# Gathering TensorE's waits and moving kept's products and the state sum in a two-stage GRU attention kernel

## The reference, cut to what is computed

```python
# first recurrence, B = 512, T = 1024, U = 64
z = sigmoid(x@Wxz + h@Whz + b); r = sigmoid(x@Wxr + h@Whr + b)
hh = relu(x@Wxh + b_in + r * (h@Whh + b_rec)); h = z*h + (1-z)*hh
logit[b, t] = sum_u(outs[t, b, u] * qw[b, u]);  a = softmax(logit, over t)
# second recurrence, its x are the first one's outs
r = sigmoid(x@Wxr + h@Whr + b); c = relu(x@Wxc + b + r * (h@Whc))
h = (1-a)*h + a*c
```

## Time and profile before

| | us |
|---|---|
| median of 3 runs (4725.99 to 4726.48) | 4726.17 |
| the profiled execution, its own time | 4727.85 |
| its span | 4726.0 |
| TensorE matmul busy | 4648.7 (98%) |
| VectorE busy | 4188.5 (89%) |
| GpSimd busy | 3629.2 (77%) |
| ScalarE busy | 2353.4 (50%) |

### The profile page before, as it was taken

How to read it: one execution, slowest core, us unless ns; L and a number is a source line. 1 busy time by engine, 2 the same in 40 slices (tenths; PEclk the granted TensorE clock), 3 DMA queues, 4 the chain that set the end, 5 groups by cost and what they waited for, 6 DMA issues and landing times.

```text
span 4726.0 us, 366111 instructions
## 1 busy us (share of the span) xinstructions
PE 4648.7 (98%) x131196; PEld 4341.8 (92%) x131196; DVE 4188.5 (89%) x28719; ACT 2353.4 (50%) x9363; POOL 3629.2 (77%) x8204
## 2 busy tenths in 40 slices
PE   8999999999999999999998999999999999999999
PEld 8999999999999999999997999999999999999998
DVE  8999999999999999999997888888888888888888
ACT  5555555555555555555553333333333333333333
POOL 6777777777777777777776888888888888888888
PEclk9999999999999999999999999999999999999999
DMA  3333333333333333333334554555555555555554
GB/s 103 107 107 114 110 107 113 110 107 111 113 107 111 113 107 108 115 108 107 115 116 119 124 122 118 124 123 119 122 124 119 121 124 120 120 124 120 119 124 108
DMA packets 169276, 544.15 MB, mean 115 GB/s; under 512 B 31644, under 2 KB 38060, under 8 KB 169260
## 3 DMA queue, kind: packets, MB, share of 16 engines
q1 hardware_dynamic: 169260, 543.93, 43.7%
HBM read 405.24 MB, written 138.56 MB: 115 GB/s over the span
## 4 chain that ended last, share of the span: by engine, by line
PE 98%; issue 1%; DMA 0%; DVE 0%; POOL 0%; SPq 0%; ACT 0%; POOLq 0%; ACTq 0%; DVEq 0%
PE r_bank_a L531 14%; PE r_bank_b L531 13%; PE c_bank_b L531 12%; PE c_bank_a L531 11%; PE logit_bank L583 6%; PE z_bank_a L537 6%; PE r_bank_a L537 5%; PE z_bank_b L537 5%; PE z_bank_a L531 5%; PE r_bank_b L537 5%; PE z_bank_b L531 4%; PE c_bank_b L537 3%; PE c_bank_a L537 3%; PE c_bank_a L543 1%; PE c_bank_b L543 1%
## 5 line engine op out<-in xcount | busy, mean ns | idle before, releaser
L295 POOL TENSOR_TENSOR kept<-z_gate,h 128x128 f32<-128x128 f32 x2048 | 931.8, 455 | 694.5 <-ACT z_gate L348 683.3
L316 POOL TENSOR_TENSOR a_kept<-attn_rest,state 128x128 f32<-128x128 f32 x2048 | 932.3, 455 | 276.7 <-POOL state L311 162.7
L311 POOL TENSOR_TENSOR state<-a_new,a_kept 128x128 f32<-128x128 f32 x2048 | 933.2, 456 | 122.0 <-DVE a_new L514 65.7
L285 POOL TENSOR_TENSOR prod<-h,qw 128x128 f32<-128x128 f32 x2050 | 933.6, 455 | 0.0
L537 PE MATMUL r_bank_a<-x,weights 64*64 64x128 f32 x8200 | 895.0, 288 | 14.0 <-ACT r_gate L377 7.9
L583 PE MATMUL logit_bank<-prod,row_sum 64*64 64x128 f32 x8208 | 895.3, 287 | 0.6 <-POOL prod L285 0.6
L537 PE MATMUL r_bank_b<-x,weights 64*64 64x128 f32 x8192 | 893.8, 288 | 0.0
L537 PE MATMUL z_bank_a<-x,weights 64*64 64x128 f32 x8200 | 876.4, 280 | 0.0
L537 PE MATMUL z_bank_b<-x,weights 64*64 64x128 f32 x8192 | 871.2, 278 | 0.2 <-DVE vec_bank L505 0.2
L444 DVE SCALAR_TENSOR_TENSOR vec_bank<-vec_bank,z_rest 128x64 f32<-128x64 f32 x4096 | 735.2, 225 | 0.3 <-issue 0.3
L455 DVE TENSOR_TENSOR h<-vec_bank,kept 128x64 f32<-128x64 f32 x4096 | 720.5, 218 | 0.3 <-issue 0.2
(11 more groups left out here) (119 smaller groups left out, 19328.3 us busy)
## 6 DMA issues: line engine op xcount, KB each, us to landing
x<-in_keys_t SPq DMA_DIRECT2D x512, 256.0 KB, 3.7
gru_outputs<-h SPq DMA_DIRECT2D x256, 512.0 KB, 3.3
x<-gru_outputs SPq DMA_DIRECT2D x512, 256.0 KB, 3.7
attn<-attention SPq DMA_DIRECT2D x512, 256.0 KB, 4.3
logits<-logit_rows SPq DMA_DIRECT2D x258, 8.0 KB
time_rows<-logits SPq DMA_DIRECT2D x2, 896.0 KB, 6.3
attention<-time_rows SPq DMA_DIRECT2D x2, 896.0 KB, 5.9
weights<-in_weight_columns SPq DMA_DIRECT2D x2, 176.0 KB, 3.7
```

Source lines behind the costliest of these rows:

```text
L285: nc.gpsimd.tensor_tensor(prod[:, (s - 1) % BODY, gcols(g)], h_at(s - 1)[:, gcols(g)], qw[:, gcols(g)], ALU.mult).then_inc(prod_ready[g], 1)
L295: nc.gpsimd.tensor_tensor(kept[:, g], z_gate[:, g], h_at(s - 1)[:, gcols(g)], ALU.mult).then_inc(kept_ready[g], 1)
L311: nc.gpsimd.tensor_tensor(state[:, (s - 1) % 2, gcols(g)], a_new[:, (s - 1) % 2, gcols(g)], a_kept[:, (s - 1) % 2, gcols(g)], ALU.add).the ...
L316: nc.gpsimd.tensor_tensor(a_kept[:, s % 2, gcols(g)], attn_rest[:, s % 2, gcols(g)], state[:, (s - 1) % 2, gcols(g)], ALU.mult).then_inc(a ...
```

## The change

In the first recurrence the slot's order becomes: [prod, xr, xz, r_ready of o, h] product for r, `gru_x_r(o)`, product for z | [z_rest of o, xh] product for the candidate, `gru_x_z(o)`, logit | [cand of o] `gru_x_h(o)`. The wait for `logits_copied` at s == 2, g == 0 stands at the front of the slot, before h's. `gru_gated` waits for rh_summed first, `gru_cand` no longer for xh_summed. In the second recurrence the slot becomes: [ar_ready of o, anew] a_new's product for r, `agru_x_r(o)`, a_new's candidate product | [axr, agated and akept of o] a_kept's two products of o | [acand of o] `agru_x_c(o)`. VectorE works in whole groups of 128 columns, and makes the state sum of the other group between gated and cand; GpSimd keeps the product alone.

```diff
@@ -303,23 +303,14 @@
                 product(BODY, g)
 
             with pool.Fori(0, T, BODY) as t0:
-                soon = t0 + 1
                 for s in range(BODY):
-                    due, soon = soon, t0 + (s + 2)
+                    done, due = t0 + (s + 1), t0 + (s + 2)
                     for g in GROUPS:
-                        pool.wait_ge(anew_ready[g], due)
-                        nc.gpsimd.tensor_tensor(state[:, (s - 1) % 2, gcols(g)], a_new[:, (s - 1) % 2, gcols(g)],
-                                                a_kept[:, (s - 1) % 2, gcols(g)], ALU.add).then_inc(s_ready[g], 1)
-                        pool.wait_ge(s_ready[g], due)
+                        pool.wait_ge(s_ready[g], done)
                         if g == 0:
-                            pool.wait_ge(rest_ready, soon)
+                            pool.wait_ge(rest_ready, due)
                         nc.gpsimd.tensor_tensor(a_kept[:, s % 2, gcols(g)], attn_rest[:, s % 2, gcols(g)],
                                                 state[:, (s - 1) % 2, gcols(g)], ALU.mult).then_inc(akept_ready[g], 1)
-            for g in GROUPS:
-                pool.wait_ge(anew_ready[g], T + 1)
-                pool.wait_ge(akept_ready[g], T + 1)
-                nc.gpsimd.tensor_tensor(state[:, (T - 1) % 2, gcols(g)], a_new[:, (T - 1) % 2, gcols(g)],
-                                        a_kept[:, (T - 1) % 2, gcols(g)], ALU.add).then_inc(s_ready[g], 1)
 
         @block.scalar
...
 
             def gru_gated(due, s, g):
+                dve.wait_ge(rh_summed[g], due)
                 dve.wait_ge(r_ready[g], due)
-                dve.wait_ge(rh_summed[g], due)
                 for part, c in PARTS:
                     nc.vector.tensor_tensor(gated[:, g, c], hid_part(g)[:, c], r_gate[:, g, c],
                                             ALU.mult).then_inc(gated_ready[g][part], 1)
@@ -430,8 +422,6 @@
                 cand, _ = vec_parts(g)
                 for part, c in PARTS:
                     dve.wait_ge(gated_ready[g][part], due)
-                    if part == 0:
-                        dve.wait_ge(xh_summed[g], due)
                     nc.vector.tensor_tensor(cand[:, c], inp_part(g)[:, c], gated[:, g, c],
                                             ALU.add).then_inc(cand_ready[g][part], 1)
...
@@ -492,37 +482,43 @@
             def agru_gated(due, s, g):
                 dve.wait_ge(ar_ready[g], due)
                 dve.wait_ge(rc_summed[g], due)
-                for part, c in PARTS:
-                    nc.vector.tensor_tensor(gated[:, g, c], c_bank[g][:, c], r_gate[:, g, c],
-                                            ALU.mult).then_inc(agated_ready[g][part], 1)
+                nc.vector.tensor_tensor(gated[:, g], hid_part(g), r_gate[:, g], ALU.mult).then_inc(agated_ready[g], 1)
 
             def agru_cand(due, s, g):
                 cand, _ = vec_parts(g)
-                for part, c in PARTS:
-                    dve.wait_ge(agated_ready[g][part], due)
-                    if part == 0:
-                        dve.wait_ge(axc_summed[g], due)
-                    nc.vector.tensor_tensor(cand[:, c], z_bank[g][:, c], gated[:, g, c],
-                                            ALU.add).then_inc(acand_ready[g][part], 1)
+                dve.wait_ge(agated_ready[g], due)
+                dve.wait_ge(axc_summed[g], due)
+                nc.vector.tensor_tensor(cand, z_bank[g][:, 0:GC], gated[:, g], ALU.add).then_inc(acand_ready[g], 1)
 
             def agru_new(due, pairs, s, g):
                 cand, _ = vec_parts(g)
-                for part, c in PARTS:
-                    dve.wait_ge(acand_ready[g][part], due)
-                    if part == 0 and g == 0 and s % CHUNK == 0:
-                        dve.wait_ge(a_loaded[s // CHUNK], pairs)
-                    last = nc.vector.scalar_tensor_tensor(a_new[:, s % 2, gcols(g)][:, c], cand[:, c], 0.0,
-                                                          attn_at(s)[:, gcols(g)][:, c], ALU.max, ALU.mult)
-                last.then_inc(anew_ready[g], 1)
+                dve.wait_ge(acand_ready[g], due)
+                if g == 0 and s % CHUNK == 0:
+                    dve.wait_ge(a_loaded[s // CHUNK], pairs)
+                nc.vector.scalar_tensor_tensor(a_new[:, s % 2, gcols(g)], cand, 0.0, attn_at(s)[:, gcols(g)],
+                                               ALU.max, ALU.mult).then_inc(anew_ready[g], 1)
+
+            def agru_sum(done, s, g):
+                dve.wait_ge(akept_ready[g], done)
+                dve.wait_ge(anew_ready[g], done)
+                nc.vector.tensor_tensor(state[:, s % 2, gcols(g)], a_new[:, s % 2, gcols(g)],
+                                        a_kept[:, s % 2, gcols(g)], ALU.add).then_inc(s_ready[g], 1)
 
             with dve.Fori(0, T, BODY) as t0:
                 pairs = t0 * PAIRS + 32
+                done = t0 + 1
                 for s in range(BODY):
                     due = t0 + (s + 2)
-                    for g in GROUPS:
-                        agru_gated(due, s, g)
-                        agru_cand(due, s, g)
-                        agru_new(due, pairs, s, g)
+                    agru_gated(due, s, 0)
+                    agru_sum(done, s - 1, 1)
+                    agru_cand(due, s, 0)
+                    agru_new(due, pairs, s, 0)
+                    agru_gated(due, s, 1)
+                    agru_sum(due, s, 0)
+                    agru_cand(due, s, 1)
+                    agru_new(due, pairs, s, 1)
+                    done = due
+            agru_sum(T + 1, T - 1, 1)
 
         @block.tensor
         def _(pe):
...
@@ -599,31 +595,32 @@
                         hs = h_at(s - 1)[:, gcols(g)]
                         o, n, due_o = 1 - g, s + g, (due, soon)[g]
 
-                        alone()
-                        pe.wait_ge(h_ready[g], due)
-                        pe.wait_ge(xr_summed[g], due)
-                        own(r_bank[g][:, 0:GC], GH_R, hs, False, True).then_inc(r_summed[g], 1)
-
                         next_chunk = g == 1 and n % CHUNK == 0
                         if next_chunk:
                             loads = count(3, t0 * PAIRS, (n // BODY + 1) * 32)
+                        i = (s - 2) % BODY
                         alone()
                         if next_chunk:
                             pe.wait_ge(x_loaded[n // CHUNK % 2], loads)
+                        if s == 2 and g == 0:
+                            pe.wait_ge(logits_copied, full)
+                        pe.wait_ge(prod_ready[g], due)
+                        pe.wait_ge(xr_summed[g], due)
+                        pe.wait_ge(xz_summed[g], due)
                         pe.wait_ge(r_ready[o], due_o)
+                        pe.wait_ge(h_ready[g], due)
+                        own(r_bank[g][:, 0:GC], GH_R, hs, False, True).then_inc(r_summed[g], 1)
                         gru_x_r(o, n)
-
-                        alone()
-                        pe.wait_ge(xz_summed[g], due)
                         own(z_bank[g][:, 0:GC], GH_Z, hs, False, True).then_inc(z_summed[g], 1)
 
                         alone()
                         pe.wait_ge(zr_ready[o], due_o)
+                        pe.wait_ge(xh_summed[g], due)
+                        own(hid_part(g), GH_H, hs, False, True).then_inc(rh_summed[g], 1)
                         gru_x_z(o, n)
-
-                        alone()
-                        pe.wait_ge(xh_summed[g], soon)
-                        own(hid_part(g), GH_H, hs, False, True).then_inc(rh_summed[g], 1)
+                        mm = logit(i, g, i == BODY - 1)
+                        if g == 1:
+                            mm.then_inc(logits_summed, 1)
 
                         alone()
                         pe.wait_ge(cand_ready[o][1], due_o)
@@ -631,15 +628,6 @@
                         if g == 0 and s % CHUNK == CHUNK - 1:
                             last.then_inc(x_used, CHUNK)
 
-                        alone()
-                        pe.wait_ge(prod_ready[g], due)
-                        if s == 2 and g == 0:
-                            pe.wait_ge(logits_copied, full)
-                        i = (s - 2) % BODY
-                        mm = logit(i, g, i == BODY - 1)
-                        if g == 1:
-                            mm.then_inc(logits_summed, 1)
-
             for i in (BODY - 2, BODY - 1):
                 for g in GROUPS:
                     pe.wait_ge(prod_ready[g], T + i - (BODY - 3))
...
@@ -703,10 +691,6 @@
                         ns = a_new[:, (s - 1) % 2, gcols(g)]
                         o, n, due_o = 1 - g, s + g, (due, soon)[g]
 
-                        alone()
-                        pe.wait_ge(anew_ready[g], due)
-                        own(r_bank[g][:, 0:GC], AH_R, ns, False, True).then_inc(ar_summed[g], 1)
-
                         next_chunk = g == 1 and n % CHUNK == 0
                         if next_chunk:
```

(24 more changed lines are left out.)

8 lines of the change are left out of this document (4 added, 4 removed).

## The result

The changed kernel takes **5019.77 us** (median of 4 runs, 5018.43 to 5021.78) against 4726.32 for the kernel before beside it: ratio 1.062, interval 1.0602 to 1.0639. It is 293 us slower, where 37 us faster was forecast; the range ended at 4980.

The account below looks back on a forecast made before the run. The loop through the state was taken to bound the first recurrence, the chain through x's and kept's products the second. Terms of -54 and +17 gave -37 against 4727.85: 4690.9 us, median 4689, 8-in-10 range 4590 to 4980.

Parts of the forecast that it names:

- items 1 and 2: First recurrence: gathered waits bring the candidate's load .07 earlier; gated waiting for rh_summed first saves .08; loop 2.32 to 2.17 us.
- Item 3: First recurrence, x's product for z behind the candidate's: slot 1.095 us, step 2.19, -133 us; ends -184 and 0.
- R2: Rival, chance .18: the first recurrence's step doesn't shorten, as xz at the front gives back the .15; +86, 4812 us.
- Item 4: First recurrence, logits_copied at the front of slot a of step 2: a stall of .695 us a body, +89 us.
- Item 5: First recurrence, a body's end: .55 us taken for today's .63, -10 us; ends -38 and 0.
- Items 6 to 8: Second recurrence: TensorE's slot 1.065 us, +17 us; VectorE's whole groups and sum, and GpSimd losing the sum, add nothing.
- Item 7: Second recurrence, VectorE: whole groups and a sum of some .28 us; loop 1.92 a step, .21 under 2.13, adding nothing.
- R1: Rival, chance .20: in both recurrences x's products wait until the own product ahead has started; +386, 5112 us.
- R3: Rival, chance .07: the second recurrence falls to its loop, 1.92 us a step; 4472 us.
- R4: Rival, chance .05: second recurrence, VectorE's sum is held for GpSimd's whole .455 us; +256 on the forecast, 4945 us.
- R5: Rival, chance .08: first recurrence, the copy's stall is absorbed if following slots run ahead on slack; 4600 us.
- The order rule: TensorE matmuls start and end in program order, so x's products load behind own products' last starts; some 5900 us; chance .01.

Follow-up runs that it names:

- Item 2 alone: The kernel before with only gated's two waits exchanged in the first recurrence, so that rh_summed is attached to the instruction: 4666.32 us (.9868).
- The exchange of products: The changed kernel with x's product for z written ahead of the candidate's own product instead of behind it: 4755.91 us (1.0056).
- The exchange of waits: The changed kernel with the front's waits for xz and prod exchanged, so that xz stands in the last wait instruction: 4732.29 us (1.001).
- the light front: The changed kernel with two wait instructions at the front, xz in the last, prod and logits_copied waiting at the slot's end before the logit: 4607.23 us (.9751).

## Why the prediction was wrong

**Bounds, items 1 and 2.** Right. gated was forecast at 1.09 - .15 = .94 of the slot and starts at +.94; the candidate's load came at +.38 for +.43. Item 2 alone brought 62 of its 82 us. A wait instruction, priced at .125, costs .105.

**Item 3 failed**, in the sentence ".33 from the last bias matmul to the released load and one more wait instruction .13: 1.09". Up to there it held: x's load for z at +.31 (forecast +.32), the last bias matmul at +.60 (+.63). From it to the front's load I counted .46 and the trace has .71. Two things were left out. First, the .33 was taken from a case in which x's product had no long own product open ahead of it; here the signal waited for that of the candidate's product, .396 from the start in place of .232, so .16. Second, with xz in the first of three wait instructions two more follow, .21 in place of .13. Together that is .25, less the .03 by which the matmul was early: the slot is 1.31 and not 1.095. Over 2048 slots this is 440 us. Two runs show the two parts one by one. The exchange of products takes .164 off the slot, the first part. The exchange of waits takes the two instructions off the route of xz; prod, with two behind it, then holds every second steady slot and more. They gave 264 and 288 us, which don't add up, since another wait takes over in each; with nothing late left ahead of the last wait instruction, the light front gives 413. I had written that both routes "nearly meet", and the dearest end of item 3 was no gain, as if xz could not be later than the old step. R2 said that xz "gives back the .15", but it too was priced at a stop at 1.16.

**Item 4.** Right in its place and its end: the front behind the copy was forecast 1.79 after the one before, and stands at 1.75. It costs .44 a body and not .695, since the slot it is measured against is longer: 56 us by the timeline, 45 by the run.

**Item 5.** Too dear. A body of the changed kernel is 8 x 2.692 = 21.54 us; 16 slots of 1.309 are 20.94, the copy .44, and .15 remain, in place of .55 for its end: 51 us less than forecast. The slot at the body's end is 1.31 like the others; the one two behind it is 1.35 and takes .04 of the .15, and the rest is scattered. Together with 440 and -33 for the copy, this leads from -54 to +302, measured +300.

**Items 6 to 8.** Right in mechanism: kept's load .65 behind x's for r (.64), x's candidate .13 behind kept's (.13), slot 1.05 (1.065), the sum .281 (.28). The term was +17 and measured -13, within its ends. Item 7's sum of the loop, 1.92 a step, was not borne out: with TensorE's cycle opened the step stopped at 2.06, and what holds it there is open.

**The rivals.** R1 had the right sign, but not the cause: x's products did not wait for the own product to start, and x's load for z stands at +.31 where R1 wanted +.44. R3 did not come. R4 had no occasion: GpSimd's product of a slot waits for the sum and ends before the next, as at 3689.49 to 3689.95 against sums at 3690.18; of 2049 sums one overlapped a product of GpSimd in the trace. All sums last 279 to 293 ns, this one 279. So whether the two engines hold each other, as the page "SBUF — State Buffer" of the Trainium skill says in its section on who interferes with whom, no run here shows. R5 did not come either: the copy's stall is there once a body.

The order rule, to which I gave .01, was half right. I had read it as one rule and dismissed it on the starts. The starts do leave the written order here too (1524.044 ahead of 1524.081), but the signals keep it. The page "TensorE: Matmul & The Clock Gate" of the Trainium skill, in Part 3 on packing small matmuls, says that matmuls keep program order both in their starts and in their ends. The runs contradict the first half for products on different blocks and bear out the second, as far as a signal tells an end; the second alone would have given the .16.

## What to carry to other kernels

Gathering waits at the front of a stage makes the stage wait for the youngest of them, and every wait instruction behind that one is paid in full: put the condition met last into the last wait instruction (read from the trace which one that is: here a wait written first can stand in the last), and leave conditions of work further down (here prod and the copy) at that work. For a signal that TensorE gives itself, count from the signals of everything written ahead, not from its own matmul. When the profile says "issue" on an engine, look for a semaphore that this engine raises itself, and for wait instructions behind it.

## What was not expected of the hardware

- The completion signals of matmuls on different blocks of the array come in written order although the starts do not: .396 us from start to signal for x's bias matmul behind an own product, .232 for the same matmul at the same time of the slot with the own product written behind it.
- A wait instruction on TensorE whose conditions are long met costs .105 in the trace where it stands behind the wait met last, and .111 a piece by 2048 of them added. Where it stands ahead of that wait, it costs nothing (the slot of the copy, 1.75 with and without it).
- On VectorE, the wait met last attached to the instruction in place of a wait instruction of its own gives back .07.
